# A two-layer graph network on one core: two more blocks of last experts in the gate's scores, seven scatters given up, a three-part sum in one operation

## The chip, the core and the metric

The kernel is one program on one NeuronCore of a Trainium2 chip. The core has TensorE (PE, with its weight loads as PEld), VectorE (DVE), ScalarE (ACT), GpSimd (POOL) and SyncE (SP), which mainly issues transfers. Time is device time in microseconds, shown as the median of three runs. A profiled execution is a run of its own, and its rows are from one execution.

## The reference, cut to what matters

There are 3125 nodes with 256 features, held as 25 blocks of 128 nodes, and 53125 edges. Layer 0 is graph attention beside a token mixer, then eight experts. Layer 1, around which the change lies, is this:

```
xn = layernorm(x)
# graph convolution: s0 = xn[src][:, :64], s1 = xn[src][:, 64:] as 64 x 3, a0 and a1 (3 parts) from edge_attr_4
out0 = s0*a0 @ w_00_0 + (sum over m of s1[..,m]*a1[m]) @ w_11_0 / sqrt(3)
out1 = s0 @ w_01_1 (x) a1 + (s1*a0) @ w_10_1
x = x + segment_sum(out * radial(edge_attr_10), dst) / 4 + mixer(xn)
xn = layernorm(x)
# gating: a second graph of 32768 edges and one loop for each node
h = xn @ W_gat;  e = leaky_relu(a_src[src] + a_dst[dst]);  alpha = segment_softmax(e, dst)
scores = layernorm(segment_sum(h[src]*alpha, dst) + b_gat) averaged over heads;  w, i = top 2 of 4 experts
x = x + sum over experts of g[e] * (gelu(xn @ W1[e] + b1[e]) @ W2[e] + b2[e])
```

## The kernel before, in words

The whole program is one sequence of stages. Within a stage each engine runs its own queue, written out by hand in the order of the work, with semaphores between the queues, and stages are separated by a barrier. There is no planner.

**Sorting the gating edges** (`sort_and_route`, line 1599). The edges with their loops lie in `pair`, 128 partitions by C2 = 288 columns. 256 columns hold edges, 25 hold loops, and the last seven hold nothing: they are filled with a number that is no node's. The place of every entry in the sorted list is computed, and each column is sent there by one indirect scatter of GpSimd. The 288 scatters are spread over five stages. `Scatter` (line 2004) issues them in turns of U = 8, and the last sixteen are issued in `mixer_matrix1` (line 2246), which computes the layer-1 token mixer's matrix on TensorE and VectorE just before the convolution. On SP's queue the sort writes zeros over the expert rows, two short pieces at the ends of the sorted list, waits for both, and goes on to load weights. ScalarE waits for those pieces before its first normed row.

**Convolution** (`convolve`, line 2323) has 55 turns of eight steps, and a step is 128 edges. For each step GpSimd gathers 128 source rows (line 2350). ScalarE scales them by the edge's four factors into `msg`, one operation over 256 columns and three over 64 (lines 2374 and 2376). TensorE multiplies `msg` by a 0/1 matrix `hot` into 512 columns of PSUM, in a ring of four (line 2363). VectorE adds the two halves of the result to the accumulator (line 2413). Once for each turn, one turn ahead, VectorE also builds `hot` (line 2389), multiplies the three parts of eight steps by their weights into `s1w` (line 2395, 1536 elements for each partition, stored as step, part, 64 columns), and sums the three parts into the last 64 columns of `msg` with two additions (lines 2400 and 2402), the second behind the first by a semaphore `chain`. Buffers: `x` four turns, `msg` and `hot` two turns.

**Gate's scores** (`gate_scores`, line 2756) has 39 turns. GpSimd gathers eight times 128 short rows of a table (line 2785), 36 numbers for each edge. SP fetches the edges' rows, TensorE spreads them over the partitions (line 2824), VectorE compares (line 2858), TensorE looks up the destination's share (line 2834), VectorE sums and stores rows and scores (lines 2866 to 2871). Beside this run the last experts of blocks 0 to 19 (EARLY = 20). A block is eight **units** on TensorE: four hidden units of 8 matrix products and four output units of 4, in the order h0 h1 y0 h2 y1 h3 y2 y3, with ScalarE's gelu between h and y of an expert. Four units go into each turn. VectorE takes each output from PSUM (line 2753) and ScalarE sends a block's outputs, 512 KB, to a table in HBM. GpSimd is **paced**: before every second gather of a turn it waits for the unit of the turn before that stands at the same place (`run.passed`), save in turn 0 and in the last turn. The last four units of block 19 have no turn beside them.

**Softmax of the scores** (`segment_softmax`) runs two more blocks (SOFT = 2). **The gate's sums** (`gate_sums`, line 2898) has 39 turns again: VectorE builds `hot` (line 2987), TensorE sums eight steps, and beside them run the last three blocks (SUMS = 3, 24 units). ScalarE cuts the summands into three bf16 parts, chunk by chunk, and `SLICED` says behind which expert's gelu each cut stands. `top_two` starts the loads of the first eight blocks from the HBM table while it picks experts. **The last stage** (`experts1`, line 3089) weighs the expert outputs block by block: first the five late blocks from SBUF, then the 20 early ones from a ring of eight slots, each slot reloaded (line 3111) once its block is done, on the queue of SP that also stores the results (line 3108).

Of the kernel before, what the change touches and what calls it, by code (L numbers as in the profile page):

```python
# [10 lines left out]
ALU = mybir.AluOpType  # L11
ACT = mybir.ActivationFunctionType
AX = mybir.AxisListType

P = 128
# [1583 lines left out]
def sort_and_route(nc, k, edge_index, pairs, pair, place_i, buf, slot_i, factor, ef, x0):  # L1599
# [11 lines left out]
    with Scope(nc) as s:  # L1611
# [64 lines left out]
        with nc.Block(no_gpsimd_drain=True) as block:  # L1676
            @block.sync
            def _(sp):
# [9 lines left out]
                sp.wait_ge(ended, 32)  # L1688
# [138 lines left out]
            def _(act):  # L1827
# [22 lines left out]
                act.wait_ge(ended, 32)  # L1850
# [153 lines left out]
class Scatter:  # L2004


    def __init__(self, s, name, first, last):
        self.first, self.turns = first, last - first
        assert self.turns % 2 == 0
        self.sent = [s.sem(name + f"sent{h}") for h in range(2)]  # L2010

# [5 lines left out]
    def run(self, nc, k, pool, pairs, pair, place_i, pace=None):  # L2017
        for i in range(self.turns):
            if i >= 2:
                pool.wait_ge(self.sent[i % 2], 16 * U * (i // 2))  # L2020
            for u in range(U):
                c = (self.first + i) * U + u
                if pace is not None:
                    for sem, count in pace(i * U + u):
                        pool.wait_ge(sem, count)
                self.one(nc, pairs, pair, place_i, i, c)
        for h in range(2):
            pool.wait_ge(self.sent[h], 16 * U * (self.turns // 2))
# [294 lines left out]
def convolve(nc, k, e, x_tab, factor, acc):  # L2323
# [4 lines left out]
    with Scope(nc) as s:  # L2328
# [10 lines left out]
        freed, built, chain, summed, added, scaled = (s.sem("cv_" + q) for q in ("freed", "built", "chain", "summed", "added", "scaled"))  # L2339
        got = [s.sem(f"cv_got{h}") for h in range(RT)]  # L2340
        with nc.Block(no_gpsimd_drain=True) as block:
# [39 lines left out]
            def _(dve):  # L2381
# [3 lines left out]
                def build(i):  # L2385
# [278 lines left out]
EARLY = T2 // U // 2 + 1  # L2664
LATE = NB - EARLY
SOFT = 2
SUMS = LATE - SOFT
assert 0 < LATE

# [86 lines left out]
def gate_scores(nc, k, e, h_tab, d_parts, rows, score, x1, xnT, y_tab):  # L2756
# [3 lines left out]
    with Scope(nc) as s:  # L2760
# [14 lines left out]
        assert turns % 2 == 1  # L2775
        with nc.Block(no_gpsimd_drain=True) as block:
            @block.gpsimd
            def _(pool):
                for i in range(turns):
                    if i >= RT:  # L2780
                        pool.wait_ge(freed, i - RT + 1)
                    for u in range(U):
                        if u % 2 == 0 and 0 < i < turns - 1:
                            run.passed(pool, (i - 1) // 2, (i - 1) % 2 * 4 + u // 2)
# [29 lines left out]
            def _(pe):  # L2814
# [23 lines left out]
                for w in range(EARLY):  # L2838
                    spread_row(w * 2 + 1)
                    fetch(w * 2)  # L2840
                    for x in range(4):
                        run.unit(pe, w, w, x)
                    spread_row(w * 2 + 2)
                    fetch(w * 2 + 1)
                    for x in range(4, 8):
                        run.unit(pe, w, w, x)

            @block.vector
            def _(dve):
# [25 lines left out]
                def keep(n, e):  # L2875
                    if n < 0:
                        return
                    if n >= 2 and e == 0:
                        dve.wait_ge(stored[n % 2], 16 * (n // 2))
                    run.keep(dve, n, e, y[:, n % 2, e, :])  # L2880
                v.memset(score[:, T2:G2 * P, :], 0.0).then_inc(took, 1)
                mark(0)
                for w in range(EARLY):
                    keep(w - 1, 2)
                    keep(w - 1, 3)
                    mark(w * 2 + 1)
                    add(w * 2)
                    keep(w, 0)
                    mark(w * 2 + 2)
                    keep(w, 1)  # L2890
                    add(w * 2 + 1)
                keep(EARLY - 1, 2)
                keep(EARLY - 1, 3)
# [4 lines left out]
def gate_sums(nc, k, e, rows, weight, acc, x1, xnT):  # L2898
# [9 lines left out]
    SLICED = {1: (1, 0), 2: (1, 1), 3: (1, 2), 6: (2, 0), 7: (2, 1), 8: (2, 2)}  # L2908
    assert chunks == 3
    POS = {2: 0, 4: 1, 6: 2, 7: 3}  # L2910
    with Scope(nc) as s:
# [11 lines left out]
        with nc.Block(no_gpsimd_drain=True) as block:  # L2923
# [26 lines left out]
            def _(act):  # L2950
# [402 lines left out]
```

## Time and profile before

| what | us |
|---|---|
| median of 3 runs | 3461.26 (3456.49 to 3465.02) |
| profiled execution, its own time | 3455.67 |
| its span | 3453.9 |
| TensorE busy | 2411.9 (70%) |
| VectorE busy | 2030.1 (59%) |
| GpSimd busy | 1704.6 (49%) |
| ScalarE busy | 1361.4 (39%) |
| profiled time outside the span | 1.8 |

The page of the profile divides the span into busy time for each engine, and its chain of waits ends in the last stage's loads. No engine is busy all through, so the shares of the whole span decide nothing here. The stages that the change touches are read one by one, by the windows view (busy time in a stretch, in the order PE, PEld, DVE, ACT, POOL), the view of waits (who waited for whom, where "issue" is idle time for which the profile has no releaser and "remote" a semaphore event that it can't place) and the timeline. In the timeline a row may stand for several merged instructions (x4), and the bracket gives the idle time before them and its releaser.

### The profile page before, as it was taken

To read this page: it belongs to the slowest core of one execution; us is meant where nothing else is said; L and a number is where in the kernel's file an instruction comes from. 1 tells how busy PE (TensorE), PEld (TensorE's weight loads), DVE (VectorE), ACT (ScalarE), POOL (GpSimd) and SP (SyncE) were. 2 spreads that over 40 slices of the span, in tenths; PEclk is the share of its full clock that TensorE was granted. 3 is DMA by queue.
4 is the path that set the end of the run, shared out by engine and by line. 5 is a ranking of instruction groups with operands and counts; after the bars stand their busy time and mean duration, and the time that the engine had idled before them with its cause. 6 is when DMAs were issued, how large, how long until landed. Compare 5 with 4: busy or idle time off the path is not lost. (4 is left out here: it accounts for less than half of the span.)

```text
span 3453.9 us, 40901 instructions
## 1 busy us (share of the span) xinstructions
PE 2411.9 (70%) x11075; PEld 1576.6 (46%) x11076; DVE 2030.1 (59%) x4071; ACT 1361.4 (39%) x3752; POOL 1704.6 (49%) x1788
## 2 busy tenths in 40 slices
PE   4995666655666765699855477777777777887775
PEld 2553444444444455565523122222236666666664
DVE  4555676767677887600083488888784622222377
ACT  0223444443444344311141478878882112111132
POOL 1545555555555203466674666666632066666200
PEclk9997777777777755599976699988898689889888
DMA  3214555555554012123130333333211111111004
GB/s 96 51 40 146 150 166 153 153 153 162 154 152 146 24 51 64 52 76 114 51 93 29 88 89 89 88 88 90 86 55 16 53 26 32 26 32 32 22 1 159
DMA packets 164936, 289.08 MB, mean 84 GB/s; under 512 B 55245, under 2 KB 99282, under 8 KB 164719
## 3 DMA queue, kind: packets, MB, share of 16 engines
q0 software_dynamic: 79568, 187.15, 19.5%
q1 hardware_dynamic: 72994, 80.59, 7.4%
q10 hardware_dynamic: 12156, 18.72, 1.5%
q8 instruction: 102, 1.67, 0.2%
q14 instruction: 116, 0.94, 0.1%
HBM read 250.08 MB, written 36.25 MB: 83 GB/s over the span
## 5 line engine op out<-in xcount | busy, mean ns | idle before, releaser
L2363 PE MATMUL cv_ps<-cv_msg,cv_hot 128*128 128x512 f32 x880 | 480.7, 694 | 212.3 <-DVE acc L2413 81.7
L961 POOL DMA_INDIRECT at_kv<-kv_tab,e_src x440 | 435.4, 990 | 382.5 <-PE at_a L1097 184.7
L2350 POOL DMA_INDIRECT cv_x<-x_tab,e_src x440 | 425.9, 968 | 228.1 <-issue 114.8
L2785 POOL DMA_INDIRECT gs_h<-h_tab,fc_q x312 | 294.3, 943 | 254.4 <-POOLq L2579 82.5
L2376 ACT ACTIVATE cv_msg<-cv_x,factors 128x64 f32<-128x64 f32 x1320 | 373.1, 335 | 113.6 <-issue 112.6
L2363 PEld LDWEIGHTS cv_ps<-cv_msg,cv_hot 128*128 128x128 f32 x880 | 181.1, 219 | 511.6 <-issue 294.3
L2413 DVE TENSOR_TENSOR acc<-acc,cv_ps 128x256 f32 x880 | 313.8, 414 | 131.1 <-PE cv_ps L2363 53.5
L2013 POOL DMA_INDIRECT pairs<-gating_pair,gating_place x288 | 282.2, 980 | 213.2 <-issue 72.9
L1072 PE MATMUL at_q<-q_parts,at_hot_n 128*128 x1320 | 242.1, 344 | 51.8 <-DVE at_kv L1154 25.9
L1097 PE MATMUL at_a<-at_kv,at_hot_e 128*128 128x264 f32 x880 | 265.4, 433 | 5.1 <-DVE at_kv L1170 5.0
L2723 PE MATMUL gs_x_y<-x_w,gs_x_hid 128*128 128x256 f32 x640 | 186.6, 440 | 98.7 <-ACT gs_x_hid L2746 76.6
L2374 ACT ACTIVATE cv_msg<-cv_x,factors 128x256 f32<-128x256 f32 x440 | 217.8, 495 | 90.5 <-DMA cv_x<-x_tab,e_src 55.7
L2746 ACT ACTIVATE gs_x_hid<-gs_x_h,x_b 128x128 f32<-128x128 f32 x320 | 90.5, 370 | 395.2 <-remote 213.2
L1181 DVE TENSOR_TENSOR acc<-acc,at_a 128x528 f32 x220 | 154.3, 702 | 126.9 <-remote 72.6
L1072 PEld LDWEIGHTS at_q<-q_parts,at_hot_n 128*128 128x128 bf16 x1320 | 154.7, 119 | 129.5 <-issue 74.3
L2723 PEld LDWEIGHTS gs_x_y<-x_w,gs_x_hid 128*128 128x128 f32 x640 | 132.1, 217 | 133.4 <-ACT gs_x_hid L2746 85.8
L1097 PEld LDWEIGHTS at_a<-at_kv,at_hot_e 128*128 128x128 f32 x880 | 171.1, 216 | 36.3 <-issue 5.0
L2713 PE MATMUL gs_x_h<-xnT,x_w 128*128 128x128 f32 x1280 | 170.7, 292 | 5.4 <-issue 5.4
L1038 ACT ACTIVATE at_fade<-at_fall 8x1 f32<-8x1 f32 x27 | 5.5, 202 | 424.5 <-DVE at_fall L1263 330.2
L2713 PEld LDWEIGHTS gs_x_h<-xnT,x_w 128*128 128x128 f32 x1280 | 166.7, 208 | 7.2 <-issue 4.1
L1154 DVE TENSOR_TENSOR at_kv<-at_kv,at_q 128x512 f32<-128x512 f32 x220 | 147.3, 680 | 27.7 <-remote 13.6
L2753 DVE TENSOR_TENSOR gs_y<-gs_x_y,x_b 128x256 f32<-128x256 f32 x80 | 33.7, 424 | 218.5 <-PE gs_x_y L2723 106.6
(547 smaller groups left out, 4624.9 us busy)
## 6 DMA issues: line engine op xcount, KB each, us to landing
x_space<-in_L_ffn_w SPq DMA_DIRECT2D x16, 1024.0 KB
at_rel_row<-e_rel_rows SPq DMA_DIRECT2D x55, 256.0 KB
experts_out<-gs_y ACTq DMA_DIRECT2D x20, 512.0 KB
x_y<-experts_out SPq DMA_DIRECT2D x20, 512.0 KB, 8.2
at_kv<-kv_tab,e_src POOLq DMA_INDIRECT x440
cv_x<-x_tab,e_src POOLq DMA_INDIRECT x440
kv_tab<-p_qkv SPq DMA_DIRECT2D x25, 256.0 KB
gs_h<-h_tab,fc_q POOLq DMA_INDIRECT x312
```

The costliest lines, as they stand in the source:

```text
L961: nc.gpsimd.indirect_dma_start(out=kv[:, t % (RING * Q4), 0:2 * D], out_offset=None, in_=kv_tab, in_offset=bass.IndirectOffsetOnAxis(ap=e. ...
L1072: ins = nc.tensor.matmul(ps_q[dd % 3][:, u, :], hot_n[:, t // Q4 % NHOT, t % Q4 * P:(t % Q4 + 1) * P], q_parts[:, ds(b, 1), n, :].rearrang ...
L1097: nc.tensor.matmul(to, hot_e[:, t // Q4 % NEDGE, t % Q4, :], kv[:, t % (RING * Q4), D:2 * D + H1], start=(u == 0), stop=(u == 1), skip_gro ...
L2013: nc.gpsimd.indirect_dma_start(out=pairs, out_offset=bass.IndirectOffsetOnAxis(ap=place_i[:, c:c + 1], axis=0), in_=pair[:, c, :], in_offs ...
L2350: nc.gpsimd.indirect_dma_start(out=xg[:, i % RT, u, :], out_offset=None, in_=x_tab, in_offset=bass.IndirectOffsetOnAxis(ap=e.src[:, t:t + ...
L2363: nc.tensor.matmul(ps[u % R][:, :], hot[:, i % 2, u, :], msg[:, i % 2, u, :], start=True, stop=True).then_inc(summed, 1)
L2374: nc.scalar.activation(msg[:, h, u, 0:D], xg[:, i % RT, u, :], ACT.Copy, scale=factor[:, t:t + 1, 0])
L2376: ins = nc.scalar.activation(msg[:, h, u, D + m * M:D + (m + 1) * M], xg[:, i % RT, u, 0:M], ACT.Copy, scale=factor[:, t:t + 1, 1 + m])
L2413: v.tensor_tensor(row, row, ps[u % R][:, n * D:(n + 1) * D], ALU.add).then_inc(added, 1)
L2713: ins = self.nc.tensor.matmul(self.ps_h[e % 2][:, f * P:(f + 1) * P], self.x1.w1[:, e, c, f * P:(f + 1) * P], self.xnT[:, c, b * P:(b + 1) ...
L2723: ins = self.nc.tensor.matmul(self.ps_y[e % 2][:, 0:D], self.hid[:, e % 2, f, :], self.x1.w2[:, e, f, :], start=(f == 0), stop=(f == FX // ...
L2785: nc.gpsimd.indirect_dma_start(out=hg[:, i % RT, u, :], out_offset=None, in_=h_tab, in_offset=bass.IndirectOffsetOnAxis(ap=e.src[:, i * U ...
```

## The change

In the sort, the seven empty columns are written to the end of the sorted list by one direct transfer on SP's queue (their places are known beforehand), and GpSimd's scatters end at column 281 (`Scatter.FILLED`). The waits for the end pieces count one more transfer. In the convolution, one `tensor_reduce` with its three inputs 64 elements apart replaces the two additions and the semaphore between them. In the gating stages, blocks 0 to 21 go into the gate's scores (EARLY = 22), 176 units spread evenly over 39 turns, so that a turn has four or five. GpSimd is paced in the last turn too. Two blocks stay in the softmax, and one (SUMS = 1) in the gate's sums, with the cuts of chunks 1 and 2 behind the gelu of experts 1 and 2. The HBM table and the last stage's loads grow from 20 blocks to 22, and the blocks kept in SBUF go from five to three.

```
+                sp.wait_ge(high, 1)
+                sp.dma_start(pairs[Scatter.FILLED * P + 1:C2 * P + 1, :]...,  pair[:, Scatter.FILLED:C2, :]).then_inc(ended, 16)
-                sp.wait_ge(ended, 32)
+                sp.wait_ge(ended, 48)
...
 class Scatter:
+    FILLED = CG + NB
+    def columns(self, i):
+        return range((self.first + i) * U, min((self.first + i + 1) * U, self.FILLED))
...
 convolve, VectorE's build(i):
-                    v.tensor_tensor(last, s1w[:, :, 0, :], s1w[:, :, 1, :], ALU.add).then_inc(chain, 1)
-                    dve.wait_ge(chain, i + 1)
-                    v.tensor_tensor(last, last, s1w[:, :, 2, :], ALU.add).then_inc(built, 1)
+                    v.tensor_reduce(last, s1w[:, :, :, :].rearrange("p u m i -> p u i m"), AX.X, ALU.add).then_inc(built, 1)
...
-EARLY = T2 // U // 2 + 1
-LATE = NB - EARLY
-SOFT = 2
-SUMS = LATE - SOFT
+SOFT, SUMS = 2, 1
+LATE = SOFT + SUMS
+EARLY = NB - LATE
...
 gate_scores:
+        def upto(i):
+            return round(EARLY * 8 * i / turns)
 GpSimd
-                        if u % 2 == 0 and 0 < i < turns - 1:
-                            run.passed(pool, (i - 1) // 2, (i - 1) % 2 * 4 + u // 2)
+                        if i and u % 2 == 0:
+                            x = upto(i - 1) + (upto(i) - upto(i - 1)) * u // U
+                            run.passed(pool, x // 8, x % 8)
 TensorE
+                for i in range(turns):
+                    spread_row(i + 1)
+                    fetch(i)
+                    for x in range(upto(i), upto(i + 1)):
+                        run.unit(pe, x // 8, x // 8, x % 8)
 VectorE
+                for i in range(turns):
+                    mark(i + 1)
+                    half = (upto(i) + upto(i + 1)) // 2
+                    if i:
+                        keeps((upto(i - 1) + upto(i)) // 2, upto(i))
+                    add(i)
+                    keeps(upto(i), half)
...
 gate_sums:
-    SLICED = {1: (1, 0), 2: (1, 1), 3: (1, 2), 6: (2, 0), 7: (2, 1), 8: (2, 2)}
+    SLICED = {1: 1, 2: 2}
...
                         if n * NX + q in SLICED:
-                            slice_off(*SLICED[n * NX + q])
+                            for m in range(3):
+                                slice_off(SLICED[n * NX + q], m)
```

## Rows read from the trace of the kernel before

**Rows 1.** Windows: stretch, length, busy us (count), clock, DMA share, GB/s; gate stages.

```profile
2765.70:3239.50 473.80, 364.85 (x2215) 298.22 (x2216) 106.95 (x268) 86.61 (x305) 294.31 (x312) 0.87 0.13 29
...
3308.00:3399.00 91.00, 72.56 (x603) 61.74 (x604) 71.21 (x68) 31.29 (x66) 0.00 (x0) 0.92 0.00 1
```

**Rows 2.** Window of 51 convolution turns; waits: total us, times, longest.

```profile
1973.50:2577.30 603.80, 438.76 (x819) 166.03 (x818) 499.05 (x1022) 485.23 (x1645) 378.63 (x391) 0.89 0.30 86
...
ACT cv_msg L2376 <- issue: 89.4, 150, 1.7
...
DVE acc L2413 <- PE cv_ps L2363: 41.2, 43, 2.8
...
DVE acc L2413 <- issue: 28.1, 40, 2.4
...
DVE acc L2413 <- DVE acc L2413: 12.0, 22, 1.0
...
ACT cv_msg L2374 <- PE cv_ps L2363: 2.9, 4, 1.1
```

**Rows 3.** VectorE groups by form: busy us, mean ns, idle before, releasers.

```profile
L2402 DVE TENSOR_TENSOR cv_msg<-cv_msg,cv_s1w 128x512 f32<-128x512 f32 x55 | 38.2, 695 | 1.9
...
L2221 DVE TENSOR_TENSOR ef_rows<-ef_angular,ef_radial_by_step 128x512 f32<-128x512 f32 x4 | 4.3, 1076 | 5.0 <-DMA ef_radial_by_step<-edge_radial,e_chunk 5.0
...
L3013 DVE TENSOR_REDUCE acc<-gu_ps 128x500 f32<-128x1500 f32 x1 | 1.7, 1720 | 3.3 <-PE gu_ps L2942 3.3
...
L3064 DVE TENSOR_REDUCE tt_q<-tt_t 128x100 f32<-128x400 f32 x1 | 0.9, 860 | 0.0
...
L3053 DVE TENSOR_REDUCE tt_r<-tt_t 128x25 f32<-128x400 f32 x1 | 0.6, 571 | 0.0
```

**Rows 4.** Timeline, start of convolution: start us, us, engine, line, operation.

```profile
1959.11 0.95 POOL L2350 DMA_INDIRECT cv_x<-x_tab,e_src  x1 [0.30 <-issue]
...
1961.82 0.35 ACT L2376 ACTIVATE cv_msg<-cv_x,factors 128x64 f32<-128x64 f32 x1 [1.05 <-issue]
```

**Rows 5.** Window of 37 gate-score turns; timeline of that stage's end.

```profile
2777.00:3222.00 445.00, 353.00 (x2165) 289.09 (x2163) 102.33 (x258) 84.60 (x300) 279.19 (x296) 0.88 0.13 29
...
3231.05 0.94 POOL L2785 DMA_INDIRECT gs_h<-h_tab,fc_q  x1 [0.30 <-issue]
...
3234.12 1.14 ACT L2746 ACTIVATE gs_x_hid<-gs_x_h,x_b 128x128 f32<-128x128 f32 x4 [16.74 <-remote]
...
3235.32 3.78 PE L2723 MATMUL gs_x_y<-x_w,gs_x_hid 128*128 128x256 f32 x8 [13.33 <-ACT gs_x_hid L2746]
...
3239.15 4.72 PE L2713 MATMUL gs_x_h<-xnT,x_w 128*128 128x128 f32 x32
...
3254.39 0.42 DVE L2753 TENSOR_TENSOR gs_y<-gs_x_y,x_b 128x256 f32<-128x256 f32 x1 [1.30 <-PE gs_x_y L2723]
```

**Rows 6.** VectorE groups of the gate's sums.

```profile
L2987 DVE TENSOR_TENSOR gu_hot<-count_row,Ws 128x1024 bf16<-128x1024 f32 x39 | 46.7, 1219 | 12.0 <-PE gu_ps L2942 11.8
...
L2753 DVE TENSOR_TENSOR x_late<-gu_x_y,x_b 128x256 f32<-128x256 f32 x12 | 5.0, 417 | 2.0 <-PE gu_x_y L2723 2.0
```

**Rows 7.** Timeline, mixer matrix: its last scatter and last step.

```profile
1898.49 0.96 POOL L2013 DMA_INDIRECT pairs<-gating_pair,gating_place  x1 [0.30 <-issue]
...
1902.27 0.76 DVE L2318 COPY G<-m1x 128x256 f32<-128x256 f32 x2 [5.54 <-PE m1x L2295]
```

**Rows 8.** Timeline of SP's queue, then of ScalarE, in the gating sort.

```profile
1251.55 1.41 SPq L2069 DMA_DIRECT2D ef_w<-in_L_gnn_fc_w  x4
...
1319.96 0.58 ACT L595 ACTIVATE r_rows<-X,shift,rstd 128x256 f32<-128x256 f32 x1
```

**Rows 9.** Last stage: timeline of VectorE and first reload; window of reloads.

```profile
3421.56 2.04 DVE L3150 SCALAR_TENSOR_TENSOR X<-x_late,gates,X 128x256 f32<-128x256 f32 x4
...
3424.34 0.43 SPq L3111 DMA_DIRECT2D x_y<-experts_out  x1
...
3436.00:3440.00 4.00, 1.99 (x8) 1.44 (x8) 2.58 (x7) 1.84 (x6) 0.00 (x0) 1.00 1.04 407
```

More of the change, by code:

```diff
@@ L1687, in _ @@
                 sp.dma_start(pairs[C2 * P + 1:(C2 + 1) * P, :].rearrange("(a r) b -> a r b", a=1), edge[:, 1, 0:P - 1, :]).then_inc(ended, 16)
-                sp.wait_ge(ended, 32)
+                sp.wait_ge(high, 1)
+                sp.dma_start(pairs[Scatter.FILLED * P + 1:C2 * P + 1, :].rearrange("(c p) b -> p c b", p=P),
+                             pair[:, Scatter.FILLED:C2, :]).then_inc(ended, 16)
+                sp.wait_ge(ended, 48)
                 sp.wait_ge(emptied, 16)
@@ L1849, in _ @@
                 act.wait_ge(emptied, 16)
-                act.wait_ge(ended, 32)
+                act.wait_ge(ended, 48)
                 row(0)
@@ L2020, in run @@
                 pool.wait_ge(self.sent[i % 2], 16 * U * (i // 2))
-            for u in range(U):
-                c = (self.first + i) * U + u
+            for u, c in enumerate(self.columns(i)):
                 if pace is not None:
@@ L2027, in run @@
         for h in range(2):
-            pool.wait_ge(self.sent[h], 16 * U * (self.turns // 2))
+            pool.wait_ge(self.sent[h], 16 * sum(len(self.columns(i)) for i in range(h, self.turns, 2)))
 class EdgeRadial:
@@ L2338, in convolve @@
         kept = s.sem("cv_kept")
-        freed, built, chain, summed, added, scaled = (s.sem("cv_" + q) for q in ("freed", "built", "chain", "summed", "added", "scaled"))
+        freed, built, summed, added, scaled = (s.sem("cv_" + q) for q in ("freed", "built", "summed", "added", "scaled"))
         got = [s.sem(f"cv_got{h}") for h in range(RT)]
@@ L2774, in gate_scores @@
         row = [s.sem(f"gs_row{h}") for h in range(2)]
-        assert turns % 2 == 1
+        POS = {2: 0, 4: 1, 6: 2, 7: 3}
+        def upto(i):
+            return round(EARLY * 8 * i / turns)
         with nc.Block(no_gpsimd_drain=True) as block:
@@ L2837, in _ @@
                 spread_row(0)
[L2838 to L2846, printed above, removed]
+                for i in range(turns):
[3 more added lines that the diff above has]
+                        run.unit(pe, x // 8, x // 8, x % 8)
             @block.vector
@@ L2875, in keep @@
                 def keep(n, e):
-                    if n < 0:
-                        return
                     if n >= 2 and e == 0:
@@ L2880, in keep, with keeps @@
                     run.keep(dve, n, e, y[:, n % 2, e, :])
+                def keeps(lo, hi):
+                    for x in range(lo, hi):
+                        if x % 8 in POS:
+                            keep(x // 8, POS[x % 8])
                 v.memset(score[:, T2:G2 * P, :], 0.0).then_inc(took, 1)
                 mark(0)
[L2883 to L2893, printed above, removed]
+                for i in range(turns):
[5 more added lines that the diff above has]
+                    keeps(upto(i), half)
+                keeps((upto(turns - 1) + upto(turns)) // 2, upto(turns))
                 dve.wait_ge(took, 1)
```

1 line of the change is left out of this document (removed).

## The prediction

> **What bounds the kernel now.** No engine is busy throughout, so I read the windows view stage by stage, then the waits of each stage that is touched, then the timeline where the waits have no named releaser. The convolution takes 603.8 us for 51 steady turns, 11.84 us each. VectorE is busy 499.05 of it, 9.79 us a turn, and ScalarE 485.23 [rows 2]. ScalarE waited for TensorE 2.9 us in all, but stood still 89.4 us in front of its three small operations with no releaser shown, and these have no wait of their own in the program. VectorE waited 41.2 us for TensorE. So ScalarE sets the pace, half of it by stalls, and VectorE follows with some slack [rows 2]. At the stage's start ScalarE issued one operation every 1.40 us (0.35 and 1.05 idle) while GpSimd issued gathers 1.25 us apart without a pause [rows 4].
>
> The gate's scores go from first gather to last turn in 473.8 us. TensorE's records fill 364.85, GpSimd's gathers 294.31 [rows 1]. Neither is full. GpSimd's floor is 0.94 + 0.30 = 1.24 us for each gather [rows 5]. In the 37 paced turns, 296 gathers need 368 us of the 445, and 77 us are stalls on the pace [rows 5]. The end of the stage shows what the pace does. In the one unpaced turn GpSimd runs until 3231.99, ScalarE stands 16.74 us and TensorE 13.33 us, and both go on at 3234 to 3235, 2.1 us after the last gather. A whole block then takes 3239.15 to 3254.39, 15.2 us, with no gather beside it, against 24 us (two turns) before [rows 5]. So this stage is held by the two together: TensorE's signals come late while gathers stream, and GpSimd must stop to receive them.
>
> The gate's sums are 91 us with VectorE 71.21 and TensorE 72.56 busy, each waiting for the other in turns [rows 1].
>
> **The sum in the convolution.** Removed are two additions of 0.695 us [rows 3], 1.39 us a turn. What one reduction of 1536 inputs costs, no row shows directly. Contiguous groups give 0.571 us for 400 inputs, and the reduction out of PSUM 1.720 us for 1500, in groups of three at a stride [rows 3]. That is 1.045 ns an input and 0.153 us fixed, so 1.76 us. But a reduction in SBUF whose inputs lie 16 bytes apart took 0.860 us for 400, 1.77 ns an input, and a product with one operand so laid out 1.076 us for 512, 1.80 ns [rows 3]. The new operation reads SBUF with inputs 256 bytes apart, so it is nearest to these: 0.153 + 1536 x 1.77 ns = 2.87 us. I take this. VectorE gets 1.48 us a turn more, 82 us over 55 turns (20 us if the cheap end holds). The removed semaphore wait was worth 0.03 us a turn, and later completion of `msg` hurts nobody, being a turn ahead.
>
> How much is on the path? VectorE's demand becomes 9.79 + 1.48 = 11.27 us a turn, and with its own gaps that have no releaser or lie between two of its additions (28.1 + 12.0 over 51 turns [rows 2], 0.79) 12.06, against 11.84 now. That gives +12 us over 55 turns if ScalarE's lead of up to 16 steps smooths everything, and +82 if nothing does. TensorE has a ring of only four results and stands while VectorE builds the next turn, which now takes 1.48 us longer. But ScalarE's lead is almost unused (2.9 us), so I take +25.
>
> The Trainium skill's page "VectorE: DVE Perf Modes", in the section on the perf-mode tier table, gives tensor_reduce a single rate for every memory, and its walkthrough names odd strides among what the plain mode takes. By that rule the reduction is the cheap one. Its page "SBUF — State Buffer" (section Door 1) says that every access to a new 16-byte line of SBUF pays a penalty, and by that it is the dear one. The 0.860 against 0.571 us for 400 inputs speaks for the second [rows 3].
>
> **The gate's scores.** Before, 148 units were passed in the 37 paced turns at 77 us of stalls, 0.52 us a unit [rows 5]. Now 38 turns are paced and 171 of the 176 units fall before the last turn: 89 us, +12. The gathers are the same 312. The end gets shorter. Today 22.8 us pass from the last gather to 3254.81. Then it is 2.1 us of release, about 2 us for a unit and the lookup, and five units at 15.2/8 = 1.9 us, 13.6 us, so -9 [rows 5]. That makes +3, and I take +5, since a fifth unit in a turn is not waited for until the next turn. The high end is that TensorE's chain keeps its 445/148 = 3.01 us a unit: 23 more units are +69, less 10 us of the old last turn and 9 at the end, +50. The low end is that the stalls stay at 77 us: -9. VectorE (102.33 of 445) and ScalarE (84.60) cover the outputs and gelus of two blocks. The two more stores of 512 KB go where the DMA share is 0.13.
>
> **The gate's sums.** TensorE loses 16 units of 1.9 us, 30 us of 72.56, and VectorE eight output additions of 0.417 us, 3.3 us [rows 6]. VectorE's 67.9 us is then the bound. Its waits for TensorE are 11.8 + 2.0 + 3.3 = 17.1 us [rows 3, 6]. I let 11.3 of them go, and add 1.6 us because the cuts of chunk 1 now stand behind the gelu of expert 1, whose units come spread out: -3.3 - 11.3 + 1.6 = -13. Ends: -20 (all go) and -3 (new waits for the cuts take their place).
>
> **The last stage.** Its middle is bound by transfers, 407 GB/s [rows 9]. Two more blocks bring 2 x (512 + 128) KB at that rate, +3.2 us. The reloads begin one pair of blocks earlier, 2.3 us before 3424.34, as that pair takes VectorE 2.04 us and some [rows 9]. Net +1, ends -1 and +4.
>
> **The scatters and the direct transfer.** Seven scatters at 1.26 us are 8.8 us of GpSimd, but its last one starts at 1898.49 and the chain of TensorE and VectorE ends after 1902.27, so nothing is won there [rows 7]. The new transfer stands before the weight loads that SP starts at 1251.55 and before ScalarE's first row to send at 1319.96 [rows 8]. That cover is 68 us, and many small pieces as on this queue cost some us. Zero, with +3 if SP's queue pushed the loads on.
>
> **Sum.** +25 + 5 - 13 + 1 = +18 us on the profiled execution's 3455.67, 3474. That run lies 5.6 us under the median, so I forecast 3479, +0.5%. About 0.3% (10 us) can be told from no change, that is 3451 to 3471.
>
> **Rivals.**
> A, cheap reduction (PSUM's rate holds in SBUF): +20 us of VectorE time within its slack, convolution +2. Sum -5, 3456. For it: groups of three at 1.045 ns. Against it: both strided SBUF rows. Chance 0.16. It is the case of the page on VectorE.
> B, the other side, faster: in the convolution, ScalarE's stalls come from GpSimd's unbroken runs of gathers [rows 4, 5]. With a slower VectorE, `freed` and the ring hold GpSimd back more often, the runs break up, and the stage runs at VectorE's 11.27 + 0.24 = 11.51 us, -0.33 x 55 = -18. Sum -25, 3436. It decides once a fifth of the 89.4 us of stalls vanishes (0.33 x 51 = 17 us). Against it: the gathers' buffers are four turns deep, so the runs stay long. Chance 0.20.
> C, the gate's scores are TensorE's chain: +50 in place of +5, 3524. For it: TensorE's wait at the end is for ScalarE [rows 5], so a chain of the two can set the pace. Against it: 15.2 us a block once gathers end. Chance 0.12.
> D, the reduction is paid in full, +82: 3536. For it: the four-deep ring. Chance 0.10.
> My forecast has 0.42, with an own range of 3466 to 3494. From these: slower by over 0.3% 0.55, within 0.3% 0.20, faster 0.25. The range for 8 in 10 runs from 3438, half of B left out, to 3530, D and the upper part of C left out.
>
> **What would show it.** Right: the reduction at 2.8 to 2.9 us in 55 records, VectorE's convolution busy time up by some 80 us with ScalarE now waiting for TensorE, turns near 12.3 us. GpSimd's stalls in the scores near 90 us and the end after the last gather near 14. VectorE's waits in the sums mostly gone and the stage near 78 us. Wrong: a reduction under 2 us, convolution turns under 11.8 us, or score turns over 13 us.

## The result and the profile after

In the first comparison the changed kernel took 3509.56 us (median of 3, 3503.23 to 3516.29) against 3461.26: ratio 1.0153, 95% interval 1.0124 to 1.0182, +48 us. Ten more executions beside the kernel before spread from 3457 to 3516 us and gave 3481.04 against 3458.32: ratio 1.0064 (1.0031 to 1.0098), +23 us. The change makes the kernel slower, and these executions spread wider too: the kernel before spread from 3447 to 3470 beside it. Here and below a ratio leaves out executions more than 1.5% above the fastest of their kernel and a median does not, so for an uneven kernel the median lies higher.

The profiled execution took 3516.29 us, 60.6 more than the profiled one of before. Read by stages (the start of each stage's first and last operations, against the same ones before), the 60.6 us come in where this table says. "Again" is the profiled execution of the ten, 3470.63 us.

```
                            first profile   again   forecast
before the convolution          +11.1        -1.1      0
convolution                     +44.9       +15.5     +25
combining, gate's rows           +0.4        +1.1      0
gate's scores                    +7.3        +2.2      +5
gate's softmax                   -0.3        +0.6      0
gate's sums                      -3.4        -3.4     -13
last stage                       +0.6        +0.2      +1
```

Three VectorE groups of the changed kernel's convolution, 51 turns (columns as in [rows 3]). They answer to the two additions there, which are gone.

```profile
L2418 DVE TENSOR_TENSOR acc<-acc,cv_ps 128x256 f32 x817 | 289.7, 414 | 123.3 <-PE cv_ps L2370 40.2 <-remote 35.0 <-issue 34.5
L2407 DVE TENSOR_REDUCE cv_msg<-cv_s1w 128x512 f32<-128x1536 f32 x51 | 97.6, 1913 | 1.7
L2402 DVE TENSOR_TENSOR cv_s1w<-cv_x,cv_factors 128x1536 f32<-128x1536 f32 x51 | 88.9, 1742 | 0.0
```

The reduction took 1.913 us, 1.15 ns an input, where I had taken 2.87 and had 1.76 as the low end. It costs VectorE 1.913 - 2 x 0.695 = 0.52 us a turn, 29 us in 55 turns. From the start of `hot` to the end of the sum, VectorE's block of building is now 4.8 us long, for 4.3 before.

The window of the same 51 turns, which answers to [rows 2], first of the first profile, then of the second.

```profile
1984.20:2634.40 650.20, 447.54 (x818) 173.23 (x817) 525.16 (x970) 491.38 (x1675) 369.22 (x391) 0.86 0.27 80
```

```profile
1971.00:2592.90 621.90, 437.46 (x817) 173.05 (x817) 525.60 (x971) 492.48 (x1679) 371.00 (x392) 0.88 0.29 84
```

VectorE is busy 525 us in both, 26 more than in [rows 2], as the reduction's price has it. Yet one takes 46 us more than the 603.8 of before and the other 18. So VectorE's own work does not set the time: one execution loses more than it, the other less. The waits say who loses. First the changed kernel's (total us, times, longest), of the first profile.

```profile
POOL cv_x L2357 <- issue: 100.0, 312, 1.9
POOL cv_x L2357 <- DVE cv_s1w L2402: 85.5, 26, 8.7
...
PE cv_ps L2370 <- DVE acc L2418: 170.8, 66, 4.3
...
ACT cv_msg L2383 <- issue: 80.4, 119, 1.8
ACT cv_msg L2381 <- PE cv_ps L2370: 49.8, 40, 3.2
```

Then the same of the kernel before, which no row ahead of the prediction shows.

```profile
POOL cv_x L2350 <- DVE cv_s1w L2395: 2.1, 6, 0.5
...
PE cv_ps L2363 <- DVE acc L2413: 81.7, 38, 3.6
```

And of the second profile of the changed kernel:

```profile
POOL cv_x L2357 <- DVE cv_s1w L2402: 19.4, 15, 7.4
...
PE cv_ps L2370 <- DVE acc L2418: 120.7, 47, 4.3
...
ACT cv_msg L2381 <- PE cv_ps L2370: 9.2, 8, 2.8
```

TensorE's waits for VectorE went from 81.7 us to 170.8 in the first profile and to 120.7 in the second. With the other causes it stood still 164.8 us before, 202.3 and 184.5 after. In its pieces the change is plainer: before, TensorE stood for more than 3 us at once ten times in the 51 turns (8 and 16 times in two profiles of experiments with the same convolution), afterwards 45 and 47 times, nearly once a turn. The other two waits belong to the first profile above all. ScalarE's cover, which I had called almost unused, is used up there: 49.8 us of waits for TensorE for 2.9 [rows 2], but only 9.2 in the second profile. And GpSimd, which before hardly waited for VectorE to release a buffer (2.1 us), does so for 85.5 us there, and for 19.4 in the second. It then issues in other rhythms, and this is where the two profiles part. The timeline shows the first.

```profile
2207.27 0.94 POOL L2357 DMA_INDIRECT cv_x<-x_tab,e_src  x1 [0.42 <-DVE cv_s1w L2402]
...
2212.73 0.35 ACT L2383 ACTIVATE cv_msg<-cv_x,factors 128x64 f32<-128x64 f32 x1 [1.04 <-issue]
...
2214.14 0.35 ACT L2383 ACTIVATE cv_msg<-cv_x,factors 128x64 f32<-128x64 f32 x1 [1.06 <-issue]
...
2214.88 0.42 DVE L2418 TENSOR_TENSOR acc<-acc,cv_ps 128x256 f32 x1 [3.06 <-issue]
...
2216.02 0.95 POOL L2357 DMA_INDIRECT cv_x<-x_tab,e_src  x1 [0.30 <-issue]
2216.17 0.30 PEld L2370 LDWEIGHTS cv_ps<-cv_msg,cv_hot 128*128 128x128 f32 x2 [3.57 <-issue]
...
2224.41 0.95 POOL L2357 DMA_INDIRECT cv_x<-x_tab,e_src  x1 [7.44 <-ACT cv_msg L2383]
```

GpSimd issued 16 gathers from 2197.2 to 2216.0, 1.25 us apart. From 2209 on ScalarE starts one operation every 1.4 us, VectorE stands 3.06 us and TensorE 3.57 us, all with no releaser, and at about 2219.7, 3.7 us after the last gather's start, all three go on at their usual rate. It is what [rows 4] showed at the stage's start. I sorted the trace's records of all profiles by it: a run is a series of gathers less than 1.45 us apart, and its stall is the time in which ScalarE's operations start 1.2 to 1.7 us apart (the stage's first run is left out).

```
                       runs of 8      runs of 12      runs of 15 or 16
before                 3:  0.9 us     6:  3.5 us      none
changed, first profile 14: 1.2 us     5:  3.9 us      8:  8.5 us
changed, again         2:  0.0 us     9:  3.9 us      2:  7.0 us
(count: mean stall of one)
```

Lengths between these are left out. Among them the kernel before has runs of 13 and 14 too, and one of 14 stalled ScalarE for 7 us, and `only_scatters`, an experiment below with the two additions kept, has one of 16 and one of 19. So long runs and stalls are not new, but with the reduction there are more of them.

With VectorE holding the buffers back, two turns' worth of gathers go out at once: in the first profile such pairs take 10.1 + 17.2 us. How much of the loss comes by this way, and how much by TensorE's ring directly, no run separates.

The gate's scores took 7.3 us more. The window that answers to the first of [rows 5], with 297 gathers, a little over 37 of the 38 turns that are now paced, and then the end of the stage:

```profile
2833.00:3302.00 469.00, 384.21 (x2385) 320.79 (x2384) 104.11 (x273) 94.42 (x336) 280.16 (x297) 0.89 0.13 30
...
3310.69 0.94 POOL L2792 DMA_INDIRECT gs_h<-h_tab,fc_q  x1 [0.30 <-issue]
...
3318.02 0.42 DVE L2756 TENSOR_TENSOR gs_y<-gs_x_y,x_b 128x256 f32<-128x256 f32 x1 [1.82 <-PE gs_x_y L2726]
```

GpSimd's stalls there are 469 - 297 x 1.24 = 101 us, and for all 38 turns (2833.7 to 3311.6) 478 - 304 x 1.24 = 101 us as well. From the end of the last gather to the end of the last output pass 6.8 us.

One profile says little about this stage. From its first gather to its last output it took 482.6 to 495.6 us in the seven profiles that keep the old gate code (the experiments below included), 489.2 in the mean, and 490.8 to 498.8 in the seven with the new one, mean 494.4. That is +5.2 us.

The gate's sums gave back 3.4 us. The window that answers to the second of [rows 1], then the waits of VectorE and TensorE in it:

```profile
3368.00:3459.00 91.00, 62.04 (x422) 49.50 (x422) 68.68 (x62) 22.57 (x35) 0.00 (x0) 0.69 0.00 1
```

```profile
DVE gu_hot L2991 <- PE gu_ps L2945: 11.7, 8, 2.8
DVE x_late L2756 <- PE m_x_y L2726: 4.1, 2, 2.9
DVE acc L3017 <- PE gu_ps L2945: 4.1, 1, 4.1
DVE gate_edge_rows L2983 <- ACT gu_part L2959: 3.8, 3, 1.7
...
PE gu_ps L2945 <- ACT gu_part L2959: 12.7, 4, 10.2
```

TensorE lost its 16 units, but VectorE's waits for it before `gu_hot` are what they were, 11.7 us for 11.8 [rows 6], and TensorE's granted clock went from 0.92 to 0.69. The waits for ScalarE's cuts were these before:

```profile
DVE gate_edge_rows L2979 <- ACT gu_part L2956: 2.1, 2, 1.0
```

This stage hardly varies: from the first `gu_hot` to the last sum it took 86.5 to 87.7 us in the seven profiles with the old code and 83.3 to 83.9 in the seven with the new.

(A correction to the part on the kernel before: an edge's gathered row in the gate's scores has 20 numbers, not 36.)

### The profile page after: what moved, and what is told of

Its sections match the earlier page's. It is cut to its first block and busy times, and to the rows that moved or that the text cites. A ratio compares the mean times of both kernels' runs of the same rounds, so it can differ in the third digit from the quotient of the medians.

```text
span 3514.5 us, 40852 instructions
## 1 busy us (share of the span) xinstructions
PE 2441.4 (69%) x11075; PEld 1595.2 (45%) x11076; DVE 2052.8 (58%) x4016; ACT 1358.9 (39%) x3752; POOL 1686.4 (48%) x1781
## 5 line engine op out<-in xcount | busy, mean ns | idle before, releaser
L2370 PE MATMUL cv_ps<-cv_msg,cv_hot 128*128 128x512 f32 x880 | 488.5, 708 | 248.8 <-DVE acc L2418 178.5
L2357 POOL DMA_INDIRECT cv_x<-x_tab,e_src x440 | 415.9, 945 | 288.7 <-issue 113.6
L2726 PE MATMUL gs_x_y<-x_w,gs_x_hid 128*128 128x256 f32 x704 | 202.0, 438 | 72.1 <-ACT gs_x_hid L2749 38.7
L2749 ACT ACTIVATE gs_x_hid<-gs_x_h,x_b 128x128 f32<-128x128 f32 x352 | 99.0, 371 | 392.9 <-remote 204.8
L2726 PEld LDWEIGHTS gs_x_y<-x_w,gs_x_hid 128*128 128x128 f32 x704 | 146.4, 218 | 102.9 <-ACT gs_x_hid L2749 58.6
L2716 PE MATMUL gs_x_h<-xnT,x_w 128*128 128x128 f32 x1408 | 185.1, 287 | 8.2 <-issue 7.7
L2861 DVE TENSOR_SCALAR gs_hot<-gs_b,count_col 128x1024 bf16<-128x1024 f32 x39 | 50.1, 1284 | 239.3 <-PE gs_b L2831 92.0
L2716 PEld LDWEIGHTS gs_x_h<-xnT,x_w 128*128 128x128 f32 x1408 | 180.3, 203 | 15.3 <-issue 11.2
```

The source lines that it names most:

```text
L2357: nc.gpsimd.indirect_dma_start(out=xg[:, i % RT, u, :], out_offset=None, in_=x_tab, in_offset=bass.IndirectOffsetOnAxis(ap=e.src[:, t:t + ...
L2370: nc.tensor.matmul(ps[u % R][:, :], hot[:, i % 2, u, :], msg[:, i % 2, u, :], start=True, stop=True).then_inc(summed, 1)
L2716: ins = self.nc.tensor.matmul(self.ps_h[e % 2][:, f * P:(f + 1) * P], self.x1.w1[:, e, c, f * P:(f + 1) * P], self.xnT[:, c, b * P:(b + 1) ...
L2726: ins = self.nc.tensor.matmul(self.ps_y[e % 2][:, 0:D], self.hid[:, e % 2, f, :], self.x1.w2[:, e, f, :], start=(f == 0), stop=(f == FX // ...
```

## The experiments

Twelve runs followed. A ratio is that of the kernel to the kernel before, run beside it on the same chip; the chips differ (the kernel before had medians of 3456, 3458, 3434 and 3457 us in the four batches of runs).

### One part at a time: `only_reduction`, `only_gate`, `only_scatters`

```diff
-v.tensor_tensor(last, s1w[:, :, 0, :], s1w[:, :, 1, :], ALU.add)
-v.tensor_tensor(last, last, s1w[:, :, 2, :], ALU.add)
+v.tensor_reduce(last, s1w[...].rearrange("p u m i -> p u i m"), AX.X, ALU.add)
...
-EARLY = T2 // U // 2 + 1
+EARLY = NB - LATE      # 22, with the new pace and sums
...
+FILLED = CG + NB       # scatters end here, one direct transfer
```

> The kernel before with one edit: the two additions of the convolution become the one reduction; scatters and gate as before. In the traces the reduction took 1.912 us against 2 x 0.695 us, 0.52 us a turn more, 29 us over 55 turns; but the convolution took 45 us more (690.3 to 735.2, first gather to last addition). Theory 1: the rest comes with the edit, because VectorE's longer building (5.03 for 4.52 us) makes TensorE stand longer, its granted clock falls oftener (187 us at the lower level in this stage before, 240 after), and GpSimd's gathers fall into unbroken runs of 16. It expects the convolution 35 to 50 us longer and the whole at ratio 1.010 to 1.014 (3496 to 3510 us). Rival: the edit costs its VectorE time only and the other 16 us are a draw of that execution: stage +29, ratio 1.008 (3490). Rival 2: most of the time lost in the convolution comes from the shifted start: stage +10 or less, ratio 1.003.

> The kernel before with the gate's edits alone: 22 blocks of the last experts in the scores' stage at the new pace, one in the sums' stage; convolution and scatters as before. Theory: the changed kernel's profile is typical, scores +7, softmax 0, sums -3, last stage +1: about +5 us, ratio 1.0015 (3466). Rival: sums bring the 13 us that I forecast, and only that execution's low granted clock there (0.69 for 0.92) hid it: -3 to -8 us, ratio 0.998 (3455).

> The kernel before with seven scatters given up and the one direct transfer in their place; convolution and gate as before. In the changed kernel's profile the convolution starts 11.1 us later, 5 of them from the attention of layer 0, whose code is the same, and 7 from the experts of layer 0. Theory: these are TensorE's clock in that execution, and this edit moves nothing: 3461, ratio 1.000. Rival: the transfer or the different queue contents cause the 11 us: ratio 1.003 (3472), with the last expert of layer 0 ending 7 us or more later.

Measured: reduction 3480.71 against 3456.45, ratio 1.0058 (1.0031 to 1.0085), 12 executions from 3450 to 3513. Gate 3459.22, 1.0009 (0.9991 to 1.0026). Scatters 3456.21, 1.0002 (0.9981 to 1.0023). So the reduction carries the loss, 24 us of median; the other two can't be told from nothing. Its ratio is under the 1.010 of theory 1 and between those of the two rivals. It is uneven too, but not alone in that: of the twelve executions of `only_scatters`, nine lie between 3450 and 3459 and three at 3480, 3503 and 3510, and none of the three was profiled. The profiled execution of `only_reduction` was its slowest and has the first profile's rhythm: 652.8 us for 51 turns, eight runs of 15 or more gathers. Over the whole stage, from first gather to last addition, the profiles with the reduction in its first place took 706, 708, 735 and 737 us, and those with the two additions there 690, 692 and 694.

`only_scatters`, the one of the three that touches what lies ahead of the convolution, started it 4.7 us earlier than before. `only_gate` started it 4.9 us earlier and `only_reduction` 7.1 later, with nothing changed ahead of it. In the seven profiles with the direct transfer the convolution starts at 1892.7 to 1915.6 us, in the mean 1904.0, in the seven without at 1899.3 to 1911.6, mean 1904.8. So the rival, that the transfer costs the 11.1 us of the first profile, falls. What makes them is open: TensorE stood at its lower clock level 7 us longer in that profile's first 500 us, but 10 us longer in those of `only_scatters` and `changed_again`, which started the convolution earlier than before.

### The whole change again: `changed_again`

No edit.

> The changed kernel once more, beside the kernel before on the same chip. The three parts alone gave medians of +24.3 us (reduction, 3450 to 3513), +2.8 us (gate) and -0.2 us (scatters), 27 us in sum; the whole change had +48.3 us in three executions each. Theory 1: the parts add up, and three executions of a kernel that scatters by 60 us were too few: ratio 1.006 to 1.009, 3478 to 3490, with a spread of 40 us or more. Rival: the parts hinder each other (the convolution starts in another rhythm): ratio 1.013 to 1.016 again.

Measured: 1.0064 (1.0031 to 1.0098), ten executions from 3457 to 3516. The parts' medians add up to 27 us, the whole has 23. The first three executions all lay at the upper end of this spread. Why those three did is open.

### Where the reduction's price comes from: `changed_close_groups`

```diff
-s1w = s.sb("cv_s1w", [P, U, 3, M])
+s1w = s.sb("cv_s1w", [P, U, M, 3])
```

> The changed kernel with the scratch of the three weighted parts laid out so that the three numbers of a group lie side by side; the reduction reads without a stride, the product writes with one of 12 bytes. The reduction took 1.912 us at a stride of 256 bytes, against my 2.87 us from rows at 16 bytes. Theory: what cost 1.77 ns an input there was inputs or results lying a short distance apart; the reduction falls to about 1.75 us (1.045 ns an input) or below, and the product, whose writes are now apart by 12 bytes, rises from 1.743 us to 1.9 to 2.8 us; in all not better, ratio 1.01 to 1.03. Rival: strides of this kind cost nothing here and both stay within 0.05 us: ratio as the changed kernel's.

Measured: 1.0127 (1.0102 to 1.0152). Its VectorE groups in the 51 turns:

```profile
L2402 DVE TENSOR_TENSOR cv_s1w<-cv_x,cv_factors 128x1536 f32<-128x1536 f32 x51 | 113.8, 2231 | 0.0
L2407 DVE TENSOR_REDUCE cv_msg<-cv_s1w 128x512 f32<-128x1536 f32 x51 | 89.4, 1753 | 1.8
```

The reduction without a stride takes 1.753 us, and with 256 bytes 1.913: the wide stride costs 0.16 us. The product that writes 12 bytes apart takes 2.231 us for 1.743, 0.49 more. So reading 256 bytes apart is cheap, writing 12 bytes apart is dear, and my estimate from reads 16 bytes apart had the wrong neighbour. One operation at several distances was not run, so that the distance alone decides is not shown. VectorE has 0.33 us a turn more than in the changed kernel; the kernel is slower, but even (3497 to 3502), with 33 of its runs just eight gathers long and hardly a stall in them (0.1 us). With a block of 5.2 us TensorE stands for more than 3 us once in every turn, 51 times. In all it stands 172 us, not much more than before, but at a granted clock of 0.82 for 0.89 its products fill 468 us for 439 [rows 2].

### VectorE's building in two pieces: `before_split_build`, `changed_split_build`

```diff
 blocks = build(i + 1)          # markers and product of the next turn
 for u, b in enumerate(blocks):
+    if u == U // 2:
+        close(i + 1)           # the additions, or the reduction
```

> The kernel before with VectorE's order in the convolution changed: the markers and the product of the next turn are made ahead of the eight tiles' additions as now, but the two small additions that end the building stand after the fourth tile. Same instructions. VectorE then keeps TensorE waiting for 2.96 us and 1.39 us in two places, not 4.5 us in one. Theory (TensorE's silences cost clock): the time at the lower clock level in the stage falls from 187 us to about 100, and each 3.4 us of it less gives about 1.6 us: convolution 20 to 45 us shorter, ratio 0.987 to 0.994. Rival (GpSimd's gathers bound it): they need 8 x 1.25 us a turn, VectorE's freer turn of 9.6 us makes their runs longer and their stalls take back what the clock gives: ratio 0.997 to 1.003, with more time in stretches of one ScalarE operation every 1.40 us than 147 us.

> The changed kernel with the same new order: markers and product ahead of the tiles, the reduction after the fourth tile (2.96 and 1.91 us in place of 4.9 us in one). Theory (clock and silences): the changed kernel's 240 us at the lower level fall to 120 or less, the convolution of 735 us to 680 to 700, ratio to the kernel before 0.995 to 1.003. Rival (VectorE's own time is what counts): the 0.52 us a turn stay and nothing is won: ratio 1.008 to 1.015.

Measured: before 0.9974 (0.9958 to 0.9989), 3451.56 against 3458.32; changed 0.9997 (0.9982 to 1.0012), executions from 3446 to 3467. The first has the ratio of its rival, though ScalarE's stalls did not grow as that had it (120 us of such gaps in the stage for 126). The second is where its theory had it. The window, then VectorE and the waits of `changed_split_build`, 51 turns:

```profile
1977.50:2578.80 601.30, 444.38 (x819) 166.79 (x818) 516.76 (x970) 481.43 (x1636) 370.47 (x391) 0.88 0.30 86
```

```profile
PE cv_ps L2370 <- remote: 80.6, 39, 3.5
PE cv_ps L2370 <- DVE acc L2424: 37.6, 32, 3.0
...
ACT cv_msg L2381 <- PE cv_ps L2370: 9.5, 15, 1.8
...
POOL cv_x L2357 <- DVE cv_s1w L2402: 4.0, 10, 1.2
```

With the same reduction of 1.907 us in it, the stage is as short as before: 601.3 us for 603.8. TensorE stands 157 us in all and for more than 3 us at once only six times, GpSimd again hardly waits for VectorE, and twelve executions lie within 22 us. That settles the place of the loss. The 0.52 us by themselves cost nothing: with the split the stage takes 601.3 us with the reduction and 600.8 with the two additions. They cost when VectorE makes them in one piece of 4.8 us while TensorE has four buffers of results. My reason for it was wrong, though. I had expected the time at the lower clock level to shrink to 120 us, and it stayed: 191 us in the stage before, 242 and 212 in the two profiles of the changed kernel, 208 and 207 with the split. The second profile of the changed kernel and the split one differ by 4 us of it and by 20 us of stage, so the clock is not what the split wins back. Where the clock falls further, as in `changed_close_groups`, it adds to the loss.

A second profile of `before_split_build` (under the label `before_split_pause`, but it has no pause):

> The kernel with the two small additions after the fourth tile once more (no pause), one look, as a second profile of that order: if its stage had the same 11.8 us a turn by chance, it comes out elsewhere than 11.6 to 12.0.

It took 11.75 us a turn after the fourth, the first profile 11.83: no chance. In the kernel before, then, the split has nearly nothing to win, since TensorE's long stands were few there (ten over 3 us).

### GpSimd's runs broken up: `before_drain`, `changed_pause`, `split_and_start`

```diff
 pool.wait_ge(scaled, t - RT * U + 1)
+if i and u == 0:                       # split_and_start: 0 < i <= RT
+    pool.wait_ge(got[(i - 1) % RT], 16 * U * ((i - 1) // RT + 1))
```

> The kernel before with one wait added in the convolution: GpSimd waits before each turn's eight gathers until its own last eight have landed, so that no run is longer than eight. Theory: ScalarE's and VectorE's unnamed stalls (ScalarE one operation every 1.40 us, 147 us of such stretches in the stage before, 174 after) come when GpSimd has issued gathers for more than some 10 us without a pause. They vanish nearly wholly, the first 60 us of the stage lose 20 to 30 us; the turns then cost GpSimd 8 x 1.25 + about 1.5 to 2 us of landing, 11.5 to 12 us, about today's 11.84. Convolution 10 to 40 us shorter, ratio 0.989 to 0.997. Rival: the runs only accompany the stalls, the stalls stay, and the wait adds its pause: convolution 20 us or more longer, ratio 1.006 or more.

Measured: 1.0095 (1.0066 to 1.0124), and in the whole stage not one ScalarE gap of 1.2 to 1.7 us, where there were 90. The first four turns took 57.8 us for 79.4. The waits of the 51 steady turns say what it cost:

```profile
POOL cv_x L2352 <- DMA cv_x<-x_tab,e_src: 131.9, 51, 2.8
...
ACT cv_msg L2376 <- DMA cv_x<-x_tab,e_src: 189.4, 51, 5.0
```

51 waits of 2.6 us (0.3 of it stands before every gather), 12.8 us a turn, and now ScalarE waits for the gathers. So the runs do cause the stalls, which the theory had right. The price of the cure was what it had wrong. (In this kernel the second gather of a turn also takes 1.31 us for 0.95, so the eight go out as two and six.)

> The changed kernel with one wait more on GpSimd: before the first gather of a turn it waits until the seventh gather of the turn before has landed. With the wait for the eighth, in the kernel before, GpSimd's next gather started 3.52 us after the last one in place of 1.25, no ScalarE gap of 1.2 to 1.7 us was left (90 in the kernel before), the first four turns took 57.8 us for 79.4, but the other turns took 12.76 us for 11.83, GpSimd now being the bound. With one landing less the pause should be about 1.0 us. Theory 1 (the stalls under long runs are what the slower VectorE brought out): no such gaps, turns of 11.3 to 11.6 us, stage 635 to 655 us for 706 to 735, ratio 0.978 to 0.988. Rival (the chain of TensorE and VectorE sets the changed kernel's turns, as where its gathers come in eights at 12.5 us a turn): no gaps, but turns of 12.2 to 12.6 us, stage 670 to 690, ratio 0.992 to 1.000.

Measured: 1.0124 (1.0088 to 1.0160). The pause of one landing less is 1.0 us where nothing else holds GpSimd back, 1.5 in the median, and the first four turns took 76.7 us. No run is longer than eight, but 74 gaps stay (106 us, 1.9 us in a run of eight). They go by the pause in front of the turn. The 24 turns behind a pause under 1.3 us have 3.6 us of stall in the mean, the ten behind 1.3 to 1.7 us have 1.4, and of the 20 behind 2.0 us or more one has a stall, of 1.4 us. So a pause of 1 us does not clear what a run leaves behind, and one of 2 us does. The 51 turns took 634.1 us, 12.4 each, and the stage 719, longer than both expectations had it. Theory 1 falls. The rival's turns are right, but not its reason alone, since gaps are left.

> The kernel before with the small additions after the fourth tile and GpSimd's wait for its own last landing before turns 1 to 4 only, where the convolution starts with 44 gathers in one run and ScalarE has a stall of some 40 us. Theory: with the wait in all turns the first four took 57.8 us for 79.4; here they do the same, the later turns keep 11.8 us, and the start's 20 us come on top of the 7 us that the new order gave: stage 660 to 668 us, ratio 0.990 to 0.994, faster than the kernel before, the changed one and the one with the new order alone. Rival: the gathers held back at the start are missed later, ScalarE never gets ahead, and the next turns give the 20 us back: ratio 0.996 to 1.000.

Measured: 0.9990 (0.9968 to 1.0011). The first four turns took 54.8 us, and then the stall came all the same: one run of 37 gathers with 32 us of gaps. The gathers held back at the start were made up in one run as soon as the wait ended. The rival was right. The lowest ratio stays that of `before_split_build`, 0.26% under the kernel before, but the two intervals overlap.

### TensorE kept busy in the gate's sums: `changed_zero_products`

```diff
 expert(i + 3)
+for q in range(4):
+    nc.tensor.matmul(ps[:, q, :], zero[:, 0:P], zero[:, :], start=False, stop=False, ...)
```

> The changed kernel with four products of zeros a turn added on TensorE in the gate's sums (36 turns, 512 columns each, they add nothing to the result). In all four profiles with 16 units of the experts taken out of this stage TensorE's granted clock there was 0.69, in the three with them 0.90 to 0.92, and the stage lost 3 us and not the 13 that I forecast. Theory: TensorE, given less to do, falls to the lower clock, each turn's products take twice as long, and VectorE waits for them as before; with the zeros the clock is at 0.85 or more again, VectorE's waits for TensorE fall by 5 us or more and the stage gets 3 to 10 us shorter. Rival: VectorE's waits have to do with the order of the work; the zeros cost TensorE time of their own and the stage gets 0 to 10 us longer.

Measured: 1.0101 (1.0065 to 1.0137) on a chip on which the changed kernel itself was not run, so the stage decides. The window, then VectorE's wait and TensorE's:

```profile
3324.50:3415.50 91.00, 75.00 (x566) 48.04 (x564) 69.28 (x64) 22.89 (x35) 0.00 (x0) 0.94 0.01 1
```

```profile
DVE gu_hot L2993 <- PE gu_ps L2945: 11.1, 12, 1.8
...
PE gu_ps L2945 <- ACT gu_part L2961: 10.2, 1, 10.2
```

The clock came back, 0.94 for 0.69, and the stage got 0.3 us shorter than in `changed_again`. VectorE's waits are 11.1 us for 11.7. So they are not a matter of TensorE's speed. The theory falls, and the stage did not get longer either, as the rival had it.

## Why the prediction came out as it did

The forecast was 3479 us, +0.5%, in a range from 3438 to 3530, with 0.55 on slower. Both medians lie in the range and on that side. The ten executions' difference of 23 us is near the forecast sum of +18, the first three's 48 is not. By parts:

**The reduction's price.** 2.87 us was forecast, 1.76 was the other end, 1.913 was measured. The term was mis-sized, 0.52 us a turn and not 1.48. The step that failed is "it is nearest to these", the rows with inputs 16 bytes apart. Against the same reduction without a stride, 256 bytes cost 0.16 us (`changed_close_groups`), and my own sign of being wrong, "a reduction under 2 us", had come true. I had cited two rules of the Trainium skill. By "VectorE: DVE Perf Modes" (tier table) one rate holds for every memory, and the trace agrees nearly: 1.15 ns an input in SBUF at 256 bytes, 1.04 there without a stride, 1.045 out of PSUM. By the line penalty of "SBUF — State Buffer" (Door 1) 256 bytes should be as dear as 16, every input lying in a line of its own, and here it was not: 1.15 ns an input against the 1.77 of [rows 3].

**What lies on the path.** I held that VectorE's demand, 12.06 us a turn with its gaps, would pass the old turn of 11.84, and took +25 between +12 and +82. The demand turned out 525.16 / 51 = 10.3 us, 11.1 with the same gaps, under the old turn. By that working the stage should have got nothing: my rival A. Yet it lost 18 us in one profile and 46 in the other. So the size of the forecast came out nearly right by luck, through two errors that cancel: a price too high (82 us of VectorE time for 29) and a loss per microsecond too low (25 of 82, where the stage lost 16 and 45 for 29). What the slack covers was worked out from VectorE's mean demand, and that step failed. The step that carried the truth was the sentence that TensorE has a ring of only four results and "stands while VectorE builds the next turn"; I had used it only for the high end. `changed_split_build` shows it: same work, other place, no loss.

**Rival B**, the faster side, had the right mechanism and the wrong sign. ScalarE's stalls do come from unbroken runs of gathers (`before_drain`: 90 gaps to none). But a later `freed` did not break the runs up, it joined two turns' gathers into one run of 16. "The gathers' buffers are four turns deep, so the runs stay long", which I had put against it, was the better guess.

**Rival C** (+50 in the scores) and **D** (+82) did not come.

**The gate's scores.** +5 forecast, +7.3 and +2.2 in the two profiles, 10.1 in that of `only_gate`, +5.2 between the means of seven and seven. Its terms in the first profile: stalls 89 us forecast, 101 measured; the end 13.6 forecast, 6.8 measured. These two misses cancel in part.

**The gate's sums.** -13 forecast, -3.4 in both profiles. The step that failed is "I let 11.3 of them go": VectorE's waits for TensorE hardly shrank with TensorE's work, 17.1 to 11.7 + 4.1 = 15.8 us, nor did they with its clock brought back. The sum of the terms as measured is -3.3 for the eight output additions, -1.3 for these waits and +1.7 for the waits for ScalarE's cuts (2.1 to 3.8, forecast +1.6), -2.9 us. That TensorE stands 10.2 us in one piece for ScalarE's `gu_part` suggests that a chain of cuts, VectorE to ScalarE to TensorE, sets the start of the stage, and that the units had only filled the time. No run changed that chain, so this is argued and not shown.

**Scatters, direct transfer, last stage.** 0 and +1 forecast; `only_scatters` 1.0002, last stage +0.6 and +0.2.

Open: what links a long run of gathers to the other engines' stalls, what makes one execution slower than the next (three of `only_scatters` were, too), and why the first three executions all lay at the upper end. Instruction loads are no likely cause of the first, as the page of the changed kernel counts few of them:

```profile
q8 instruction: 102, 1.67, 0.2%
q14 instruction: 115, 0.94, 0.1%
```

## What to carry to other kernels

When one engine's operations stand together in one block in front of a neighbour with few buffers, look at the length of the block, not at the engine's share: half a microsecond more in a block of 4.3 cost 18 to 46 us over 51 turns here, and the same work split in two cost nothing. Count the neighbour's long stands in the trace, not only its total. Take the price of a strided operation from a row of the same operation with the same distance in bytes. And run an uneven kernel ten times before its difference is put down to anything: three executions gave +48 us where ten gave +23.

## What the runs showed of the hardware

GpSimd's gathers, issued every 1.25 us without a pause, bring the other engines to a stand after about ten: runs of 8 stalled ScalarE for 0 to 1.2 us, of 12 for 3.5 to 3.9, of 15 and 16 for 7 to 8.5, at one ScalarE operation per 1.4 us. Pauses of 2.3 us after every eighth clear it wholly (`before_drain`). In `changed_pause` runs of eight behind pauses under 1.3 us keep 3.6 us of stall, and those behind 2.0 us or more next to none. The Trainium skill's page "SBUF — State Buffer", in the section on its two separate sides, has it that only the port pair shared by GpSimd and VectorE causes waiting on the engines' side and that ScalarE and TensorE never wait on anyone. These engines do stand here, with no releaser, whatever the cause; no run shows that a port is it.

On VectorE a reduction of 1536 inputs in SBUF took 1.753 us without a stride and 1.913 with its inputs 256 bytes apart, and a product of 1536 took 1.743 us written without a stride and 2.231 written 12 bytes apart.

TensorE's granted clock can fall because work was taken from it: 0.92 to 0.69 in the gate's sums, and the same in all six profiles without the 16 units and the zeros, and back to 0.94 with products of zeros, with next to nothing in time by it (0.3 us).
